# Experts' results scaled on the way out of PSUM and added to the output by accumulating scatters

## What is computed

```python
x = x + cross_attention(layernorm(x), ctx)      # 16 heads, 4096 keys per batch
x = x + window_attention(layernorm(x))          # window of 64
t = layernorm(x)
probs = softmax(t @ Wr + br)                    # 16 experts ("banks")
topv, topi = top_k(probs, 2)                    # two experts per token
h = relu(t @ W1[e] + b1[e])                     # 256 -> 1024
y = h @ W2[e] + b2[e]                           # 1024 -> 256
x = x + sum over the two experts of topv * y
```

## Time and profile before

| | us |
|---|---|
| median of 3 runs | 1291.03 (1286.94 to 1292.49) |
| the profiled execution | 1287.06 |
| its span in the profile | 1285.2 |
| TensorE busy (12182 matmuls) | 1232.0 (96%) |
| VectorE, ACT, POOL busy | 863.3, 719.0, 258.4 |
| DMA | 148.34 MB, 115 GB/s on average |

### The profile page before, as it was taken

The page is one execution under the profiler, slowest core; times in us unless marked ns, Lnnn a source line. Parts: engine busy times, 40 slices in busy tenths (PEclk is TensorE's granted clock), DMA queues, the critical chain, the costliest instruction groups (busy, mean ns, idle before and its releaser), DMA issues.

```text
span 1285.2 us, 29573 instructions
## 1 busy us (share of the span) xinstructions
PE 1232.0 (96%) x12182; PEld 702.3 (55%) x12182; DVE 863.3 (67%) x1648; ACT 719.0 (56%) x942; POOL 258.4 (20%) x255
## 2 busy tenths in 40 slices
PE   8989999999999999999999999999999998999994
PEld 5454444555544455544445554444556567787774
DVE  5978888766787967688886667993365675232233
ACT  4557777676677766677776667777433321121220
POOL 4322112211112211112211111202012242222210
PEclk9989999999999999999999999999999997999997
DMA  7833673543455543344753433511000007999983
GB/s 221 133 50 58 86 168 52 75 61 58 58 108 113 86 69 57 50 57 100 134 78 51 57 51 57 82 20 52 8 2 2 2 34 275 407 410 395 393 337 112
DMA packets 47622, 148.34 MB, mean 115 GB/s; under 512 B 16816, under 2 KB 20928, under 8 KB 39552
## 3 DMA queue, kind: packets, MB, share of 16 engines
q1 hardware_dynamic: 43232, 134.57, 44.4%
q0 software_dynamic: 2528, 7.38, 1.8%
q10 hardware_dynamic: 1728, 4.49, 1.0%
HBM read 87.68 MB, written 5.24 MB: 72 GB/s over the span
## 4 chain that ended last, share of the span: by engine, by line
PE 87%; DVE 5%; ACT 4%; issue 2%; DMA 1%; POOL 1%; ACTq 0%; DVEq 0%; POOLq 0%
PE psum L629 21%; PE psum L611 15%; PE psum L589 11%; PE psum L503 7%; PE psum L522 6%; PE psum L1059 5%; PE psum L1087 4%; ACT wts L1132 2%; PE psum L1084 2%; PE psum L1053 2%; PE psum L707 2%; DVE part_max L1372 2%; PE psum L827 1%; PE psum L701 1%; PE psum L657 1%
## 5 line engine op out<-in xcount | busy, mean ns | idle before, releaser
L1382 DVE TENSOR_REDUCE part_max<-psum 128x1 f32<-128x512 f32 x952 | 609.9, 686 | 166.0 <-PE psum L589 164.5
L1132 ACT ACTIVATE wts<-psum 128x1024 f32<-128x1024 f32 x512 | 515.9, 1023 | 92.6 <-PE psum L611 91.7
L629 PE MATMUL psum<-wts,vals 128*17 128x256 f32 x4096 | 317.3, 385 | 0.0
L611 PE MATMUL psum<-queries,keys 51*128 51x256 f32 x2048 | 261.2, 333 | 7.9 <-ACT wts L1132 7.0
L611 PEld LDWEIGHTS psum<-queries,keys 51*128 51x128 f32 x2048 | 158.3, 185 | 199.4 <-issue 141.5
L589 PE MATMUL psum<-keys,queries 51*128 51x512 f32 x1024 | 227.7, 440 | 11.4 <-ACT wts L1132 6.0
L629 PEld LDWEIGHTS psum<-wts,vals 128*17 128x17 f32 x4096 | 69.6, 95 | 120.5 <-issue 96.4
L589 PEld LDWEIGHTS psum<-keys,queries 51*128 51x128 f32 x1024 | 97.3, 184 | 30.6 <-DVE part_max L1372 11.3
L1811 POOL CAST key_high<-key_low 128x1024 fp32r<-128x1024 f32 x31 | 32.2, 1038 | 396.5 <-ACT key_low L1139 392.2
L522 PE MATMUL psum<-wv,ctx_in 64*128 64x256 f32 x768 | 101.4, 394 | 2.1 <-ACT vals L1145 1.3
L1302 ACT ACTIVATE hid<-psum,b1s 128x128 f32<-128x128 f32 (+1 forms) x124 | 31.7, 350 | 112.0 <-PE psum L1059 75.6
(11 more groups left out here) (244 smaller groups left out, 1005.5 us busy)
## 6 DMA issues: line engine op xcount, KB each, us to landing
keys<-key_high SPq DMA_DIRECT2D x256, 128.0 KB, 4.3
w1s<-in_W SPq DMA_DIRECT2D x31, 1024.0 KB
w2s<-in_W SPq DMA_DIRECT2D x31, 1024.0 KB
keys<-key_low SPq DMA_DIRECT2D x128, 128.0 KB, 6.1
ctx_in<-in_ctxT SPq DMA_DIRECT2D x12, 768.0 KB, 8.6
ctx_in<-in_ctxT ACTq DMA_DIRECT2D x4, 768.0 KB, 12.6
queries<-query_high SPq DMA_DIRECT2D x60, 32.0 KB, 5.0
rows_x<-xn SPq DMA_DIRECT2D x2, 512.0 KB, 2.6
```

Source lines behind the costliest of these rows:

```text
L611: m = e.matmul(bank(S_BANKS[S_NO["s", n] % 2] + i)[:, hh * SEQ:(hh + 1) * SEQ], keys[64 * i:64 * i + STK, hh, c, at:at + P], queries[g % 3 ...
L629: i = e.matmul(bank(O_BANK)[32 * j:32 * j + VW, 0:SEQ], vals[:, t, h * VW:(h + 1) * VW], wts[n % NW][:, j * SEQ:(j + 1) * SEQ], start=(t = ...
L1132: i = e.activation(wts[n % NW], s_bank(job, 2), ACT.Exp, scale=QSCALE)
L1382: e.reduce_max(part_max[g % 2][:, hq, c:c + 1], bank(M_BANKS[n % 3]), AX_X).then_inc(dve_max, 1)
```

## The change

The results of the experts don't go through scratch any more. VectorE multiplies each result by its rows' gates as it takes it out of PSUM, and POOL scatters it with an addition in the DMA (`compute_op=ALU.add`) straight into the output. For that:

- The output has 128 spare rows behind its 1024, for empty places (`aside` has their numbers). ACT stores x, with the biases, to it before the experts start, and a copy of x's first rows to the spare ones (`st_x`). POOL waits for both before its fourth gather.
- A gate per row and tile is needed: POOL makes `gate_tile` (in_tile times the gates), TensorE multiplies `at_row` by it in 16 fp32 matmuls, in place of the 32 of `keep_busy`, VectorE copies that to `gate_row`.
- Two tiles may hold the same token, and a split tile the same token in both halves. So every addition waits until all earlier ones have landed (one semaphore, `st_y`), and a split tile is added in two transfers, in each of which the other half's rows go to the spare rows (`to_half`). That makes 31 additions for 24 tiles. VectorE waits with result j for the additions of tile j-3.
- The read-back, the weighing and the last stores are gone.
- Apart from that, `PER_STEP` is 850, value jobs 12 and 13 are done in the lead-in and 14 and 15 two steps earlier, and POOL waits for the eighth weighing (pe_pv) before it adds the bias.

```diff
@@ -84,9 +84,9 @@
              ("q", 1), ("v", 0, 8), ("v", 0, 9), ("k", 3), ("v", 0, 10),
-             ("v", 0, 11)]
+             ("v", 0, 11), ("v", 0, 12), ("v", 0, 13)]
 LEAD_SIZE = {"v": (3, 512), "turn1": (1, 896), "q": (4, 768), "k": (3, 1024)}
-PER_STEP = 770
+PER_STEP = 850
@@ -104,7 +104,7 @@
 LEAD_PIECES, FIRST_AT = lead_pieces()
-FIRST_AT.update((2 * j - 23, [("v", 0, j)]) for j in range(12, KT // 2))
+FIRST_AT.update((2 * j - 25, [("v", 0, j)]) for j in range(14, KT // 2))
...
@@ -458,9 +460,9 @@
-        def y_stored(i, upto):
-            return 16 * len(range(i, upto, YRING))
+        def y_added(j):
+            return 16 * (j + split_no(j))
@@ -1016,7 +1018,12 @@
             biases(range(TT // 2, TT))
-            keep_busy(32, 4)
+            e.wait_ge(pool_gtile, 1)
+            for n in range(2 * TT):
+                i = e.matmul(bank(4)[:, 0:TILES], at_row[:, n].bitcast(F32), gate_tile[:, n],
+                             start=(n == 0), stop=(n == 2 * TT - 1))
+            i.then_inc(pe_grow, 1)
@@ -1074,6 +1081,8 @@
                     e.wait_ge(dve_y, j - 1)
+                else:
+                    e.wait_ge(dve_grow, 1)
                 dst = bank(4 + j % 2)[:, 0:EMB]
@@ -1285,6 +1294,11 @@
+            e.wait_ge(dve_b2, TT // 2)
+            e.dma_start(out[0:TOK].rearrange("(p i) e -> p i e", i=TT), x).then_inc(st_x, 16)
+            e.dma_start(out[TOK:], x[:, 0]).then_inc(st_x, 16)
             for j in range(TILES):
@@ -1302,13 +1316,6 @@
                 i.then_inc(act_h, 1)
-            by_pair = scratch["rows_y"][0:2 * TOK].rearrange("(c p i) e -> p c i e", c=2, i=TT)
-            for i in range(YRING):
-                e.wait_ge(st_y[i], y_stored(i, TILES))
-            for b in range(BATCH):
-                e.dma_start(picked[:, TT + b * BT:TT + (b + 1) * BT], by_pair[:, 1, b * BT:(b + 1) * BT]).then_inc(
-                    ld_y[b], 16)
@@ -1737,9 +1744,17 @@
             e.tensor_scalar_max(from_row, second, 0.0).then_inc(dve_from, 1)
-            e.scalar_tensor_tensor(spare, pair, 0.0, spare_no, ALU.is_equal, ALU.mult).then_inc(own.up(), 1)
+            e.tensor_scalar(spare, pair, 0.0, aside[:, 0:1], ALU.is_equal, ALU.mult).then_inc(own.up(), 1)
             e.wait_ge(dve_seq, own.n)
-            e.scalar_tensor_tensor(to_row, pair, -1.0, spare, ALU.add, ALU.add).then_inc(dve_to, 1)
+            e.tensor_tensor(to_rowf, second, spare, ALU.add).then_inc(own.up(), 1)
+            e.wait_ge(dve_seq, own.n)
+            e.tensor_copy(to_row, to_rowf).then_inc(dve_to, 1)
+            e.tensor_scalar(in_half, to_rowf[:, FULL:], aside[:, 1:2], None, ALU.subtract).then_inc(own.up(), 1)
+            e.wait_ge(dve_seq, own.n)
+            for half in range(2):
+                e.tensor_scalar(to_half[:, half], in_half, aside[:, 2 + half:3 + half], aside[:, 1:2],
+                                ALU.mult, ALU.add).then_inc(dve_to, 1)
             for i in range(TT // 2):
@@ -1777,10 +1792,15 @@
                 if j >= YRING:
-                    e.wait_ge(st_y[j % YRING], y_stored(j % YRING, j))
-                e.tensor_copy(yout[j % YRING], bank(4 + j % 2)[:, 0:EMB]).then_inc(dve_y, 1)
+                    e.wait_ge(st_y, y_added(j - YRING + 1))
+                e.tensor_scalar(yout[j % YRING], bank(4 + j % 2)[:, 0:EMB], gate_row[:, ORDER[j]:ORDER[j] + 1], None,
+                                ALU.mult).then_inc(dve_y, 1)
             for s in range(TILES + 2):
+                if s == 1:
+                    e.wait_ge(pe_grow, 1)
+                    e.tensor_copy(gate_row, bank(4)[:, 0:TILES]).then_inc(dve_grow, 1)
+                    e.wait_ge(dve_grow, 1)
                 if s < TILES:
@@ -1789,16 +1809,6 @@
                     hidden(s - 1)
-            e.wait_ge(dve_b2, TT // 2)
-            for b in range(BATCH):
-                e.wait_ge(ld_y[b], 32)
-                for c in range(2):
-                    for i in range(b * BT, (b + 1) * BT):
-                        if c:
-                            e.wait_ge(dve_out, 2 * b * BT + i - b * BT + 1)
-                        e.scalar_tensor_tensor(x[:, i], picked[:, c * TT + i], gates[:, i, c:c + 1], x[:, i],
-                                               ALU.mult, ALU.add).then_inc(dve_out, 1)
@@ -1890,6 +1900,7 @@
                 if n == 0:
+                    e.wait_ge(pe_pv, 8)
                     e.wait_ge(ld_w, 16 * 4)
@@ -1945,6 +1956,9 @@
                             ALU.mult).then_inc(pool_attile, 1)
+            e.tensor_tensor(gate_tile.rearrange("p (c t) n -> p c t n", c=2), in_tile.rearrange("p (c t) n -> p c t n", c=2),
+                            gates.rearrange("p t (c o) -> p c t o", o=1).broadcast_to([P, 2, TT, TILES]),
+                            ALU.mult).then_inc(pool_gtile, 1)
@@ -1954,21 +1968,28 @@
-            def store_rows(j):
+            def add_rows(j, half=0):
+                t = ORDER[j]
+                to = to_half[:, half, t - FULL:t - FULL + 1] if split(j) else to_row[:, t:t + 1]
                 e.wait_ge(dve_y, j + 1)
-                e.indirect_dma_start(scratch["rows_y"], bass.IndirectOffsetOnAxis(ap=to_row[:, ORDER[j]:ORDER[j] + 1], axis=0),
-                                     yout[j % YRING], None).then_inc(st_y[j % YRING], 16)
+                if j or half:
+                    e.wait_ge(st_y, y_added(j) + 16 * half)
+                e.indirect_dma_start(out, bass.IndirectOffsetOnAxis(ap=to, axis=0), yout[j % YRING], None,
+                                     compute_op=ALU.add).then_inc(st_y, 16)
                 load_rows(j)
-            e.wait_ge(dve_to, 1)
+            e.wait_ge(dve_to, 3)
+            e.wait_ge(st_x, 32)
             for s in range(TILES + 2):
                 if s >= 2:
-                    store_rows(s - 2)
+                    for half in range(2 if split(s - 2) else 1):
+                        add_rows(s - 2, half)
...
@@ -2062,15 +2083,8 @@
-            by_pair = scratch["rows_y"][0:2 * TOK].rearrange("(c p i) e -> p c i e", c=2, i=TT)
-            for i in range(YRING):
-                e.wait_ge(st_y[i], y_stored(i, TILES))
-            for b in range(BATCH):
-                e.dma_start(picked[:, b * BT:(b + 1) * BT], by_pair[:, 0, b * BT:(b + 1) * BT]).then_inc(ld_y[b], 16)
-            for b in range(BATCH):
-                e.wait_ge(dve_out, 2 * BT * (b + 1))
-                e.dma_start(out[:, b * BT:(b + 1) * BT], x[:, b * BT:(b + 1) * BT]).then_inc(st_o, 16)
-            e.wait_ge(st_o, 16 * BATCH)
+            e.wait_ge(st_x, 32)
+            e.wait_ge(st_y, y_added(TILES))
@@ -2140,7 +2154,7 @@
         "pair_no": (1 + TOK * (np.arange(2 * TT)[None, :] // TT) + TT * p[:, None] + np.arange(2 * TT)[None, :] % TT).astype(f),
-        "spare_no": (2 * TOK + 1 + p[:, None] + P * np.arange(TILES)[None, :]).astype(f),
+        "aside": np.stack([TOK + 1 + p, TOK + p, p < H, p >= H], 1).astype(f),
         "before": (p[:, None] < p[None, :]).astype(f),
...
```

23 lines of the change are left out of this document (12 added, 11 removed).

## The result

The change made the kernel slower: 1334.68 us (median of 4 runs, 1330.89 to 1337.81) against 1289.62 (4 runs, 1286.94 to 1292.49), a ratio of 1.0348, 95% interval 1.0309 to 1.0386. Forecast were 1293.0 and a range up to 1314. The profiled execution has a span of 1329.1 us against 1285.2, 43.9 more, at a granted clock of 0.969.

The account below looks back on a forecast made before the run. TensorE's chain was taken to bound the kernel, DMA engines full beside it. 22.6 additions at 7.3 us from 1093.8, then 28.6 us for the rest, gave span 1287.2; with run offsets, 1293.0 us, range 1273 to 1314.

Parts of the forecast that it names:

- the price of a link: Experts' stage: each of 31 chained additions takes 7.3 us beside the weights' loads and 3.4 us after them.
- I take 0.7: Additions: an accumulating scatter takes 0.7 us more than a plain one, 0.40 for its read and 0.3 for longer descriptors.
- The start: Start of the experts' results: first addition at 1093.8 us, from 1096.8 less 3.6 for the front plus 0.6 for routing.
- The three result buffers let the chain lag by some three tiles: Experts' stage: past that lag VectorE waits with a result, TensorE behind it, and TensorE's stage is late; no separate size.
- The traffic term: Experts' DMA: 14.0 us of extra traffic plus 2.9 for x's store, less 5 of slack, moves TensorE's end by 12 us.
- some 7 us: End of the experts' stage: how far weight loads run ahead of their use; 5 us taken, with 0 and 8 as ends.
- The chain at its dear price: Experts' stage: the target's read waits again in the loaded queue, 10.9 us per addition, 3.1 after; 1313.7 us, chance 0.29.
- The sum made by the page: Additions: by the skill's 2 us per HBM access at high load, 0.2 after it, the same sum gives 1298.8 us.
- The clock: Experts' stage: chain stalls idle TensorE and a third runs at the low clock, adding 29 us; about 1322 us, chance 0.06.
- The front: Before and in the main loop: moved value jobs and POOL's later bias additions make it 3.6 us faster, bounds 1 and 6.
- The four small operations: VectorE at the first maxima: without POOL's bias additions beside them they fall to 0.17 to 0.18 us, 1.7 us less.
- moved value jobs: Lead-in and main loop: two value jobs leave the loop, 4.1 us, and cost 2.2 us earlier; net 1.9 less, between 0 and 5.

Follow-up runs that it names:

- free plain writes: Changed kernel with plain scatters into six separate scratch targets, so none waits for the one before, results left out of the output: 1281.19 us, 0.9930 of the kernel before.
- chain of plain writes: Changed kernel with plain scatters into the output in place of accumulating ones, each still waiting for the one before: 1295.19 us, 1.0031 of the kernel before.
- adds_free: Changed kernel with accumulating scatters into six separate scratch targets, so none waits for the one before, results left out of the output: 1286.56 us, 0.9978 of the kernel before.
- before_pv: Kernel before with only POOL's wait for the eighth weighing ahead of its bias addition: 1287.58 us, 0.9978 of the kernel before.
- before_front: Kernel before with only the change's front: step budget 850, moved value jobs and the wait on the eighth evacuation: 1288.27 us, 0.9989 of the kernel before.
- deep_both: Changed kernel with 16 result buffers for 3, 10 row buffers for 5 and gathers seven tiles ahead for three: 1323.36 us, 1.0260 of the kernel before.

## Why the prediction was wrong

**What held.** The end of the old kernel (16.8 us of TensorE's silence) did go: with free plain writes the last result is issued at 1273.70 and the span ends at 1279.6. That POOL would wait for landings and not for VectorE, that VectorE would wait for the additions' semaphore, and that additions would run on after the last matmul, all of it is in the rows, though 7 of POOL's 30 waits are put down to VectorE, four of whose results had waited for a buffer. That the additions form a chain and that it reaches TensorE was the forecast's; the price of a link was not, and the way over POOL's queue was missing.

**The step that failed: the price of a link, and in it "I take 0.7" for what an addition costs beyond a scatter.** The forecast had 7.3 us a link beside the weights and 3.4 without them; measured were 9.4 and 4.5. The landing of a plain scatter was right (6.3 and 2.4; in the chain of plain writes about 6.4 and 2.5). Two terms were too small. From a landing to the next issue the forecast had 0.3 us, the gap between issues that wait for nothing; behind a wait it was 0.7. And accumulation adds 2.3 us beside the weights, and 1.35 without (4.55 less 3.2), in place of 0.7. Without them, 0.6 is POOL's own instruction, 1.57 for 0.97, and the rest is about what the packets move longer, 1.35 us for 0.44. The price had been put near the low end because its read cost 0.40 elsewhere; but that was a transfer's share of the engines' time, and what counts here is how long one transfer takes from issue to landing. Whether the 2.3 us beside the weights come from the 128 packets in place of 32 or from the read of the target, no run separates.

The forecast's own sum with the measured prices: from 1093.8 to the weights' assumed end at 1258.5 there are 17.5 links, 13.5 x 4.5 = 60.8 follow, 1319.4. That is 32 of the 41.9 us by which the span was missed (1329.1 - 1287.2); the gap behind a landing alone would make about 8 of them.

**The start.** First addition at 1103.5, forecast 1093.8. The same sum from there gives 16.5 + 14.5 links and 1323.9, 4.5 more. In these 9.7 us are 3.2 from what stands ahead of the routing (VectorE's owner numbers came 0.4 earlier, not 3.6), 3.9 from the routing's clock, 2.0 from gather to first expert (2.6 later, not 0.6; the gate matmuls took 7.02 us, all at the clock's lower level, where 5.24 had been reckoned from rows that were partly at the upper) and 0.7 from there to the first result. With deep buffers, where only the chain counts, the span was 1321.9.

**What late buffers cost, and the end.** Of the remaining 5.2 us, 1.9 stand at the end: the span ends 6.5 us after the last addition's issue, 3.8 to its landing and 2.7 more, where the sum has 4.6 in all. What holds the end for the 2.7 the runs don't tell. For the other 3.3: the chain's price was charged on a weights' stream of fixed length. In fact a stalled TensorE holds weight buffers, the stream stretches to about 1285, and dear links still fall beside its end (three from 1258.72 to 1286.06, 9.1 us each). "The three result buffers let the chain lag by some three tiles; then VectorE waits" was right, but nothing was charged for it, and the gathers behind a waiting addition in POOL's queue were not seen at all. They belonged to the question of what is queued behind a new wait on its engine.

**The traffic term** was wrong in the other direction. The forecast had TensorE's end moved 12 us by it. In adds_free, which has all of this traffic, TensorE needs 189.1 us for the stage, against 185.2 before: 4, not 12; and with plain writes it needs 185.0, so the fourth write and the store of x cost nothing that shows. (The slack of the weights, "some 7 us", is 8.2 by its own rows, 1257.73 less 1249.5.)

**The rivals.** The chain at its dear price was the right one of the four, at 0.29, though its prices were wrong both ways: beside the weights it had 10.9 us for measured 9.4, and without them 3.1 for 4.5. It gave 1313.7, 21 short. With the measured prices the same sum gives 11.5 us more; the rest is the late start, the stretched stream and the end, as above. The Trainium skill (DMA: Bandwidth & Descriptors, "Latency and other measured facts"), with 2 us for an HBM access at high load, is near this case beside the weights: 2.3 us, the difference of 9.4 and 7.1, or 1.7 without the 0.6 of POOL's instruction. Its 0.2 us average does not account for the 1.35 found on idle DMA engines, nor for the 0.75 that are left of it without POOL's instruction. The sum made by the page, 1298.8, was as low as it was since it stood on the same plain prices (6.6 and 2.7) and left the unloaded links at 2.9.

The clock: that rival's 1322 is the nearest number of the four, but by luck. The clock fell in the stage as it says, but for 30.8 us and not a third of 185 (1169.4 to 1183.1, 1230.9 to 1244.5, 1278.6 to 1282.1), and TensorE stood for 18 of them. On the chain that ended last it lengthened one expert's 32 passes from 3.57 to 5.82 us. It goes with the chain's stalls: with two chains its mean was 0.983, for 0.969 in the changed kernel and 0.987 before.

**The front** was predicted at 3.6 (1 to 6); by itself it gave 1.7, in an interval from 3.2 less to 0.4 more, which leaves out the 3.6 and takes in no gain at all. The four small operations did fall to 0.17 to 0.18 us (L1397 after, L1390 before):

```profile
L1397 DVE CAST neg_parts<-neg_max x16: 178/179/180, 70.3 to 867.4; 128x8 bf16<-128x8 f32 x16
```

That is the part which is seen to survive, and before_pv has most of it: there three of the four fall, and the first still takes 0.48 us, beside POOL's split of a key and not beside the bias. The 1.9 us from moved value jobs are not to be seen: the stretch at the lower clock only moved, from 73.2 to 80.0 to 77.2 to 84.0, and caught a value job again (2.46 us, for the 2.56 of the earlier trace rows). TensorE was busy for 5.59 of the 6.80 us in the first and 6.04 in the second, so it was not half idle before, as the expectation of before_front has it.

## What to carry over

Where transfers must wait for one another, price the link, not the transfer: from issue to landing in the state of the queues in which it will run, plus the time from a landing to the issue that waits for it (0.7 us here, not the 0.3 between issues that wait for nothing), times the number of links, against the time in which the producer makes as many results. If the product is longer, deeper buffers only move the wait (11 of 45 us here); two targets with a chain each, five buffers and one merge took 42 of 45. And of every wait put into an engine's queue, ask what unrelated issue stands behind it. A tail that is taken away has to be weighed against the finer-grained dependence that replaces it: 16.8 us of read-back went, 30 waits came, and even with two targets the change only came level with the kernel before (1.0009 and 1.0015).

## What the runs showed of the hardware

An accumulating indirect transfer of 128 rows of 1 KB went as 128 packets where the plain one went as 32 of 4 KB; its instruction held POOL 1.57 us in place of 0.97, its landing came 3.7 us after the issue at the least (3.5 in deep_both), against 2.4, and as one link of a chain it took 4.5 us alone and 9.4 beside the weights (all queues together at some 370 to 390 GB/s), against 3.2 and 7.1. Of each link 0.7 us lay between the landing and the issue that waited for it. A plain accumulating transfer of 1 MB from one array in HBM to another took POOL 1.01 us to issue and held its target 8.6 us, in a stretch with no other load:

```profile
q0 software_dynamic: 272, 1.05, 63.1%
```

The row is the DMA view of that stretch. Its 256 data packets of 4 KB moved at about 205 GB/s (most slices of that stretch show 186 to 223), half of the 407 GB/s that the stage's traffic reaches.
